# Sixteen filler transposes, one chunk moved up and one maximum split in a graph-attention kernel

## The reference, cut to what matters

```
x, adj: (8192, 128), (8192, 8192), float32        # adj is added as the mask
h      = max(layernorm(x), 0)
proj   = einsum('nf,hfo->hno', h, W)               # 4 heads
scores = leaky_relu(s_src[:, :, None] + s_tgt[:, None, :], 0.2)
attn   = softmax(adj[None] + scores, axis=1)       # down the columns of adj
vals   = elu(einsum('hij,hjo->hio', attn, proj) + h[None])
out    = x + vals.mean(axis=0)
```

## Time and profile before

| | us |
|---|---|
| median of 3 runs | 935.72 |
| lowest and highest run | 931.46, 936.46 |
| the profiled execution | 935.8 |
| its span, first to last instruction | 934.1 |
| busy in the span: DVE | 805.6 (86%) |
| busy: PE (weight loads apart) | 710.0 (76%) |
| busy: ACT | 682.9 (73%) |
| busy: POOL | 288.6 (31%) |
| reading of memory, mean over the span | 315 GB/s |

### The profile page before, as it was taken

How to read it: one execution, slowest core, us unless ns; L and a number is a source line. 1 busy time by engine, 2 the same in 40 slices (tenths; PEclk the granted TensorE clock), 3 DMA queues, 4 the chain that set the end, 5 groups by cost and what they waited for, 6 DMA issues and landing times.

```text
span 934.1 us, 14971 instructions
## 1 busy us (share of the span) xinstructions
PE 710.0 (76%) x4995; PEld 576.0 (62%) x4995; DVE 805.6 (86%) x812; ACT 682.9 (73%) x1173; POOL 288.6 (31%) x164
## 2 busy tenths in 40 slices
PE   1507687987887987988987987888898888838882
PEld 1506576776776776777776766776686776613330
DVE  3886888999988999988999999999988995429996
ACT  0498577977977977977977887887886887755552
POOL 1000202332332232432232432432332422227885
PEclk8657989999999999999999999999999999969997
DMA  9999999999999999999999999999999996853112
GB/s 250 332 375 392 373 346 372 348 366 375 370 360 374 350 368 374 372 360 372 354 367 372 373 370 369 374 370 371 372 369 354 363 278 147 222 116 98 56 46 58
DMA packets 224100, 294.93 MB, mean 316 GB/s; under 512 B 4544, under 2 KB 218048, under 8 KB 224064
## 3 DMA queue, kind: packets, MB, share of 16 engines
q1 hardware_dynamic: 214848, 290.27, 90.7%
q0 software_dynamic: 9216, 4.20, 3.7%
HBM read 281.80 MB, written 12.65 MB: 315 GB/s over the span
## 4 chain that ended last, share of the span: by engine, by line
PE 36%; issue 16%; ACT 13%; DVE 12%; DMA 11%; POOL 6%; SPq 4%; ACTq 0%; POOLq 0%; DVEq 0%
PE ps L446 27%; ACT ps L517 12%; PE ps L414 7%; DMA sums<-arena 6%; DMA arena<-in_adj 5%; DVE arena L597 5%; POOL arena L400 4%; DVE ps L602 3%; SPq L343 3%; DVE arena L580 3%; POOL arena L404 2%; SPq L328 1%; PE ps L433 1%; DVE arena L601 1%; PE ps L421 1%
## 5 line engine op out<-in xcount | busy, mean ns | idle before, releaser
L517 ACT ACTIVATE ps<-ps,arena 128x1024 f32<-128x1024 f32 x512 | 556.1, 1086 | 180.7 <-DVE arena L601 110.6
L446 PE MATMUL ps<-ident,arena 128*128 128x128 f32 x4096 | 560.4, 285 | 75.9 <-ACT ps L517 57.9
L446 PEld LDWEIGHTS ps<-ident,arena 128*128 128x128 f32 x4096 | 463.8, 145 | 161.9 <-ACT ps L517 137.9
L580 DVE TENSOR_TENSOR arena<-arena 128x3072 f32<-128x3072 f32 (+2 forms) x115 | 359.3, 3125 | 13.3 <-DMA arena<-in_adj 10.2
L387 POOL DMA_INDIRECT sums<-arena x64 | 175.6, 2744 | 530.3 <-DVE arena L636 230.7
L414 PE MATMUL ps<-ident,arena 128*128 128x128 f32 x512 | 75.2, 295 | 104.0 <-DVE ps L602 61.8
L414 PEld LDWEIGHTS ps<-ident,arena 128*128 128x128 f32 x512 | 62.6, 152 | 111.0 <-issue 67.2
L597 DVE TENSOR_REDUCE arena<-ps 128x1 f32<-128x1024 f32 x64 | 78.4, 1225 | 45.5 <-PE ps L414 43.7
L517 ACT ACTIVATION_READ_ACCUMULATOR ps<-ps,arena 128x1 f32 x512 | 100.5, 196 | 0.0
L576 DVE TENSOR_TENSOR arena<-arena 128x3072 f32<-128x3072 f32 (+2 forms) x23 | 71.8, 3124 | 14.7 <-DMA arena<-in_adj 14.7
L602 DVE SCALAR_TENSOR_TENSOR ps<-ps,arena 128x1024 f32<-128x1024 f32 x64 | 82.1, 1282 | 0.3 <-issue 0.3
(11 more groups left out here) (74 smaller groups left out, 184.0 us busy)
## 6 DMA issues: line engine op xcount, KB each, us to landing
arena<-in_adj SPq DMA_DIRECT2D x160, 1536.0 KB, 14.5
arena<-in_adj SPq DMA_DIRECT2D x16, 512.0 KB, 7.2
arena<-in_adj SPq DMA_DIRECT2D x8, 1024.0 KB, 8.5
sums<-arena SPq DMA_DIRECT2D x1, 4160.0 KB, 22.4
arena<-sums SPq DMA_DIRECT2D x8, 512.0 KB, 7.2
out<-arena SPq DMA_DIRECT2D x16, 256.0 KB, 2.3
sums<-arena POOLq DMA_INDIRECT x64, 8.4
w_sb<-in_L_gnn_W SPq DMA_DIRECT2D x1, 256.0 KB, 2.9
```

The costliest lines, as they stand in the source:

```text
L446: mm = pe.transpose(turned_ps[n % 2][:, m, :], piece(i, r, nq)[:, m, q * P:(q + 1) * P], ident[:, :])
L517: act.activation(turned_ps[n % 2], turned_ps[n % 2], ACT.Exp, scale=KAPPA, bias=cert[:, i, q, G:G + 1], accum_out=cert[:, i, q, r:r + 1]). ...
L580: dve.tensor_tensor(acc_of(nq), acc_of(nq), piece(i, r, nq), ALU.max).then_inc(f_acc, 1)
```

## The change

It has four parts.

1. **Fill** (`FILL` = 16). Behind `turn_maxima(0)` of a strip of three sets PE runs 16 transposes of the identity into `idx_ps`, whose content is dead at that place. They wait for nothing and nothing waits for them but PE's own next instruction.
2. **Order** (`FRONT`). In strips of three sets the chunk (0,2) moves from place n = 6 to n = 5, and (2,1) from 5 to 6.
3. **Split.** For the strips 2 to 20, `piece_max(1)` (128x3072) becomes two instructions: `first_set_max`, set 0 alone (128x8x128), which stands in the strip before between `find_rows` and `column_max(2)`, and the other two sets (128x8x256) at the old place.
4. A new semaphore `f_acc0` lets `piece_max(2)` wait for both halves.

```
-        return [(r, q) for q in range(nq) for r in range(LEAD)] + ...      (for nq == 3)
+    FRONT = [(0, 0), (1, 0), (2, 0), (0, 1), (1, 1), (0, 2), (2, 1), (1, 2), (2, 2)]
+    FILL = 16
...
+    def split(g, i):
+        return subs(g, i) == NQ and (not known(g) or number(g, i) >= 2)
...
+        if nq == NQ:
+            return FRONT + [(r, q) for r in range(LEAD, G) for q in range(nq)]
...
                 turn_maxima(g, i, 0)
+                if nq == NQ:
+                    for n in range(FILL):
+                        pe.transpose(idx_ps[:, n % NQ, :], ident[:, :], ident[:, :])
                 for n in range(EARLY, nq * G):
...
                 if r == 1:
+                    cols = slice(P if split(g, i) else 0, nq * P)
                     dve.wait_ge(f_in[slot(i, 0)], landed(g, i, 0))
                     dve.wait_ge(f_in[slot(i, 1)], landed(g, i, 1))
-                    dve.tensor_tensor(acc_of(nq), piece(i, 0, nq), piece(i, 1, nq), ALU.max).then_inc(f_acc, 1)
+                    dve.tensor_tensor(acc_of(nq)[:, :, cols], piece(i, 0, nq)[:, :, cols], piece(i, 1, nq)[:, :, cols],
+                                      ALU.max).then_inc(f_acc, 1)
                 else:
                     dve.wait_ge(f_in[slot(i, r)], landed(g, i, r))
+                    if r == 2 and split(g, i):
+                        dve.wait_ge(f_acc0, Q - 1)
...
+            def first_set_max(g, i):
+                nq = subs(g, i)
+                dve.wait_ge(f_in[slot(i, 0)], landed(g, i, 0))
+                dve.wait_ge(f_in[slot(i, 1)], landed(g, i, 1))
+                dve.tensor_tensor(acc_of(nq)[:, :, 0:P], piece(i, 0, nq)[:, :, 0:P], piece(i, 1, nq)[:, :, 0:P],
+                                  ALU.max).then_inc(f_acc0, 1)
...
                     if q == nq - 1 and not first_strip(g, i):
                         find_rows(*before)
+                    if q == nq - 1 and not last_strip(g, i) and split(*after):
+                        first_set_max(*after)
                     column_max(g, i, q)
```

More of the change, by code:

```diff
@@ L207, in peaked_path @@
     f_acc = sem("pieces_max")
+    f_acc0 = sem("first_set_of_two_pieces_max")
     f_max = sem("substrip_max")
```

## The result

The changed kernel takes 940.12 us (median of 13 runs, 938.73 to 944.88) where the kernel before takes 936.0 on the same chips. The ratio is 1.005, with a 95% interval of 1.0034 to 1.0065: slower by half a per cent, 3 to 6 us. The profiled execution takes 938.73 us, its span is 936.6.

A forecast was written before the change was run, and what follows sets the result against it. The loop through ACT and PE was taken as the bound, DVE 0.2 us ahead. Strips 3 to 19 +7.1, strip 20 +0.67, early strips -1.2: total +6.6, 942.3 us; range 936 to 952.

The forecast's parts named there:

- The two hand-over rows: Trace rows between strips: DVE's first maxima ready at about 536.26, PE starting turn_maxima(0) at 536.47, so DVE 0.2 us ahead.
- DVE is the bound: Rival for the steady strips: DVE's path sheds 0.67 us a strip, 11 us, giving 913; chance 0.04.
- the delay is taken up: Rival within a strip: exponentials behind chunk 5 close up at 1.1 us each, not 1.2, giving 924; chance 0.09.
- the pace of 2.39 us for two chunks: Within a strip, chunk 7's exponential starts 2.39 us after chunk 5's, since a turn waits for the exponential two back.
- the late reduce: DVE's third reduce in a strip, behind first_set_max: predicted to end 0.41 us late, and the bias with it.
- The whole 10.7 us: Clock loss in strips 3 to 19, 592.3 us against 581.6 at 34.21 each; the fillers were predicted to recover it all.
- the base of 34.21: Length in us of a good strip at full clock, to which the prediction added 1.05 for each of strips 3 to 19.
- The clock rivals: Two rivals on PE's clock: fillers don't keep it (951.5, chance 0.10), or its loss moves elsewhere in the strip (951, 0.09).
- It moves to the new gap: Rival: PE's new 1.5 us idle, chunk 7 waiting for exponential 5, loses the clock in seven strips, 951; chance 0.09.
- the gap of 2.93 us: PE's idle before the second turned maxima of a strip; fillers were to leave 1.1 us of it.
- It stays as it is: Rival: the fillers don't keep PE's clock, seven strips stay slow, +15.8 us, 951.5; chance 0.10.
- Early strips: Strips 1 and 2: chunk 5 of strip 1 7.5 us late but covered by ACT's idle; 1.2 us gained overall.

## Why the prediction was right, and where it was off

**What bounds the strip.** Right. The two hand-over rows that placed DVE 0.2 us ahead of ACT and PE held: DVE relieved of 0.7 to 0.8 us brought nothing in the strips with the old order (928.15 to 926.97, strips 585.8 to 586.4), 0.68 us more on it cost 0.29 under the fillers and nothing in the changed kernel. The rivals "DVE is the bound" and "the delay is taken up" are out; the second with the pace of 2.39 us for two chunks, which stayed. (That rival counted 17 pairs of chunks behind chunk 5. There are nine, which at 0.19 us each would still have taken up the whole delay.)

**Order.** 0.67 us predicted, 0.65 measured in the kernel with fillers and order.

**Split.** Another 0.41 was predicted for the late reduce, 0.24 to 0.35 measured (0.29 on average). The step that was mis-sized is the duration: I ended `find_rows` at 510.65 and let `first_set_max` run 1.2 us from there. DVE started it 0.07 us behind the start of the last tiny operation and the reduce 1.15 us behind that. By the same sum DVE was relieved of 3.35 - 2.29 - 0.24 = 0.82 us in strip 13, not 0.67. Strips came out at 35.13 and not 35.26, which is 2.2 us of the 17.

**Fill.** The clock rose to 1.00 in every strip and the second turned maxima to 1.06, as predicted. The whole 10.7 us were rightly in this sum, for a reason that it didn't give: the strips had become so long that the loads could follow. Alone the fillers bring 6.3 us in the strips, and 8 in all, because the loads come at 34.46 us a strip. The prediction noted that DMA was full and left it out of the base of 34.21.

**The clock rivals.** "It moves to the new gap" is out: PE idles 1.31 us behind chunk 6 and no strip lost the clock. The Trainium skill (TensorE: Matmul & The Clock Gate, "HAM oscillation") lays lost clock at idle gaps between bursts of matmuls; the traces agree in kind for the gap of 2.93 us, since no strip lost the clock once it was filled, and show that two gaps of 1.2 and 1.3 us a strip are harmless here. "It stays as it is" did not happen with the fillers, but its price was wrong. It kept the count of seven slow strips, 951.5; without fillers order and split take 956.5, as 14 strips are slow. That count was a term held constant without a reason.

**Early strips.** Strip 1 waited for its load as foretold. Its `first_set_max` starts after 8.08 us of idle and chunk 5 is 7.2 us late (7.5 predicted):

```profile
89.81 1.23 DVE L603 TENSOR_TENSOR arena<-arena 128x1024 f32<-128x1024 f32 x1 [8.08 <-DMA arena<-in_adj]
92.40 1.09 ACT L529 ACTIVATE ps<-ps,arena 128x1024 f32<-128x1024 f32 x1 [9.47 <-DVE arena L625]
```

ACT's idle at the strip's end covered it. From the first exponential of strip 1 to that of strip 3 the kernel gained 1.4 us (1.2 predicted), while the first one came 0.9 later, which no part of the change reaches.

**The sum.** In the span: +0.9 at the start, -1.4, +5.1 (7.1 predicted), +0.6 for strip 20 (0.67), and -2.7 from strip 21 to the end, of which the prediction had nothing: 1.8 of them are the clock of strip 21, and 0.9 in the tail stay unexplained. Together +2.5 in the profiled spans and 3 to 6 us in the ratio, against +6.6. Neither the 1.8 nor the 0.9 at the start belongs to the change as far as the runs show, so part of how the total came out is chance. The 35.13 us a strip are not: every strip of the changed kernel lies within 0.13 of it.

## What to carry to other kernels

Cost a part by where it sits in the loop that closes last, found at the hand-over from one round to the next; DVE was busy for 95% of a strip and still not on it. When a consumer is moved ahead by one place, look at what it waits for besides its data: here a bias that arrives late. And value a part together with its neighbours: the same fillers were worth 8 us in one kernel and 16 in another, since the loads cap the gain in the one, and in the other 14 strips and not seven had lost the clock.

Of all the versions the fillers alone are the simplest fast one, 0.992 of the kernel before; the split with the old order brings 0.990, and moving the first turned maxima ahead of chunk 1 as well 0.988. What stands in their way, at 371 GB/s, is the reading of `adj`.

## What was not expected of the hardware

- The clock's loss is steep. With PE idle for 2.93 us ahead of the second turned maxima, 6 of 17 strips were slow in the kernel with the split alone, 7 in the kernel before, 11 with the order (34.85 us in its good strips), 14 with order and split, and 17 with 0.68 us more on DVE, whose strips take 34.7 us where the clock holds and in which PE idles another 0.3 us or so. The 2.93 was the same in good strips and in slow ones; what decides which strip loses the clock was not settled. With 1.18 us of idle none did.
- Four kernels with different orders, one of them with a shorter compute loop, all end at 371 GB/s (365 for the loads alone, in pieces of 1.5 KB), 34.5 us for the 12.6 MB of a strip.
